# Attention scores in three bursts instead of four, value products together, and maxima turned at full width

## The chip, the cores and the metric

The kernel runs on one core of one Trainium2 chip. The time is the device time of one execution in microseconds (us). The median of three executions is 664.26 us, with 659.87 and 670.34 as the ends. One of its executions was also recorded by the hardware profiler; all rows below are from that one.

## The reference, cut to what matters

Two layers are computed on x of shape (4, 512, 512), fp32. The change is in the first one:

```python
xn = layernorm(x)
q = rope((xn @ wq).reshape(4, 512, 32, 16)); k = rope((xn @ wk).reshape(4, 512, 8, 16)); v = xn @ wv
scores = einsum('bqhd,bkhd->bhqk', q, repeat(k, 4)) / sqrt(16)   # causal mask added
s = einsum('bhqk,bkhd->bqhd', softmax(scores), repeat(v, 4)) @ wo
y_all = relu(einsum('bsd,edh->bseh', xn, W_e) + b_e)             # 8 experts, the top 2 of a token are used
x = x + s * silu(mean of the two chosen experts' rows)
```

There are 32 query heads and 8 key heads in each of 4 batches. The second layer (a long convolution and a linear gate) follows and is not touched.

## The kernel before, in words

**Groups.** The attention is done in 32 groups (b, h): one batch and one key head, with its 4 query heads. Group number i is 8b + h. The causal scores of a group are computed twice. The first time (`scores_1`, L1569, matmul L1591) they have the queries on the partitions, only so that the row maxima can be found; the second time (`scores_2`, L1596, matmuls L1617 and L1620) they have the keys on the partitions, with the negative maximum of each query added by two extra rows of the contraction, so that the exponential can be taken at once. Each of the two halves fills 10 PSUM banks' worth of work, n = 0 to 9. The first half goes round 3 banks (`S1_BANK`), the second round 3 others (`S2_BANK`). So `scores_1` number n may only start when the maxima of number n - 3 are out of the bank (the wait on `b_m`, L1584), and `scores_2` number n when the exponentials of number n - 3 are done (the wait on `b_e`, L1606). The contraction has 48 or 50 rows, and the two halves lie on different 64 rows of the array (`first_half` chooses them), so that one of each half can run side by side: a pair.

**Who does what.** VectorE takes the maxima (`maxima`, L1377, one L1390 instruction for each query head and tile, with a read of its accumulator behind it), turns the finished output of the group before (`rows_of`), divides it (`normalise`) and turns two groups' output for the projection (`pair_rows`). It also turns the expert tiles' gathered tokens (`expert_x`, L1458) and does a share of the second layer's preparation (`dve_s4`). ScalarE does the exponentials (`exps`, L1514) and the experts' relu (L1524). GpSimd zeroes the masked part of the diagonal blocks (`select`, L1332) and gathers tokens.

**The maxima of a group** go a long way round. After the tenth bank of maxima VectorE makes two negated fp32r parts (`maxima_parts`, L1403 and L1405), TensorE turns them into the first bank set (`turn_maxima`, L1628, called T below), VectorE copies 32 rows out (`maxima_rows`, L1413), and two DMAs, one issued by SyncE and one by ScalarE (`maximum_rows`, L1315), put the rows under the queries. `scores_2` number 0 of that group waits for both (`b_mr`, L1601).

**The order on TensorE** is written out by hand in `go` of `pe_b` (L1700). In the loop turn of group g, `following` is g + 1 and `after` is g + 2. A burst is a row of pairs. Between bursts stand quarters: a quarter is one of the 4 contraction steps of an expert tile (`expert`, L1672) or an output projection (`project`, L1683), as two fp32 matmul instructions of 512 columns; the first quarter of an expert tile has a short bias matmul in front (L1670). All these use bank 7, so a new tile waits until ScalarE has emptied it (`bank_free`). Between bursts lie the gaps 0 to 4; how many quarters stand in each gap of each group is `SIZES`: 6 and 8 by turns.

```python
scores(e, (2, 3, 4), following, (0, 1, 2), (b, h));  quarters(b, h, 0)     # burst A
scores(e, (5, 6, 7), following, (3, 4, 5), (b, h));  quarters(b, h, 1)     # burst B
scores(e, (8, 9), following, (6, 7), (b, h))                               # burst C
values(e, b, h, 0);  quarters(b, h, 2);  turn_maxima(e, *following)
scores(e, (0, 1), after, (8, 9), (b, h));  quarters(b, h, 3)               # burst D
for j in ORDER[1:]: values(e, b, h, j)
quarters(b, h, 4)
```

`values` (L1644) multiplies the exponentials with the values; four matmuls of 32 output rows run side by side.

**The stacks.** Queries and keys of two groups at a time are loaded by 12 DMAs (`load_stacks`, L1308 and L1309), issued by SyncE in every odd h, in order behind the stores of expert tiles, the shuffles of tokens and `maximum_rows`. They wait until the scores of the current group are all issued and done (`b_s2`, L1292), because they overwrite its buffer, and are needed by `scores_1` number 0 in the last burst of the next group (`b_ld`, L1578). This is already so in the kernel before, and `load_stacks` itself is not in the diff.

Of the kernel before, what the change touches and what calls it, by code (L numbers as in the profile page):

```python
# [21 lines left out]
F32 = mybir.dt.float32  # L22
# [54 lines left out]
def times_of(k):  # L77

    return {UNITS[n][1]: 4 * (b * KV + h) + min(gap, 3) for (b, h, gap), quarters in WORK.items() for n, q in quarters
            if q == k and UNITS[n][0] == "x"}  # L80
# [7 lines left out]
def turns():  # L88

    first, last, at = times_of(0), times_of(KB - 1), {}  # L90
    for m in range(MT):
        t = first[m] - 2 + m if m < 2 else max(first[m] - 2, last[m - 2])
        t += -1 if t % 2 == 0 and (m < 2 or t > last[m - 2]) else t % 2 == 0
        assert t < first[m]
        at.setdefault((t // (4 * KV), t // 4 % KV, t % 4 // 2), []).append(m)
    return at
# [24 lines left out]
for _name, _n in (("ident", P), ("half", 1), ("eps", 1), ("minus", 1), ("mask", S), ("tri", P), ("cos", TPB * 8), ("sin", TPB * 8), ("s4", 16),  # L121
                  ("lower", E * E), ("i128", NT), ("i128m", MT + 1), ("tile", MT), ("iota", P), ("tilenum", TOPK * NT), ("part", 1), ("sel", E)):
# [6 lines left out]
def constants():  # L129
# [26 lines left out]
    put("minus", -1.0)  # L156
    put("sel", np.arange(E)[None, :] == p[:, None] % 32)
# [58 lines left out]
def build(nc, x_d, wq_d, wk_d, wv_d, wo_d, wg_d, bg_d, we_d, be_d, lam_d, p_d, q_d, vct_d, ct_d, bp_d, dd_d,  # L216
          step_d, wft_d, sc_d, bf_d, const_d, dft_d, out_d):
    ctx = ExitStack()
    with ctx:
# [56 lines left out]
        NAR = 18440  # L276
# [186 lines left out]
        def dve_a(e, st):  # L463
            v = nc.vector
            v.memset(ones_b[:, :], 1.0).then_inc(a_ones, 1)
            v.memset(be3[:, :], 0.0).then_inc(dve_steps, st.one())
            e.wait_ge(a_load, 16)
# [76 lines left out]
            def rope(b, u):  # L544
                if due(at := 4 * (nth(b, u) - 1)):
                    e.wait_ge(a_add[u % 2], at)
                if (b, u) == LAST:
# [4 lines left out]
                    maxima_rows(e, 0, 0)  # L552
# [23 lines left out]
            def sequence(b, more):  # L576
                for u in range(TPB):
# [5 lines left out]
                    if (b, u) == LAST:  # L583
                        maxima_parts(e, st, 0, 0)
# [38 lines left out]
            maxima_parts(e, st, 0, 1)  # L623
            maxima_rows(e, 0, 1)
            dve_experts(e, st)
            for n in (0, 1):
# [192 lines left out]
        def pool_a(e, st):  # L819
# [12 lines left out]
            def constant_columns():  # L832
# [3 lines left out]
                g.memset(kt[32:64].bitcast(F32), 1.0).then_inc(b_init, 1)  # L836
                e.wait_ge(b_init, 1)
                g.memset(kt[96:P].bitcast(F32), 1.0).then_inc(b_init, 1)
# [142 lines left out]
        def pe_a(e):  # L981
# [89 lines left out]
            scores(e, (0, 1), (0, 2), (), None)  # L1071
# [136 lines left out]
        m_parts = parts("m_parts", [P, 2, 2, HALF * TPB], "arena", used[0])  # L1208
        take([P, 2, 2, HALF * TPB])
        m_rows = take([P, P])[0:2 * 2 * HALF * TPB]  # L1210
# [100 lines left out]
        def maximum_rows(e, b, h, s):  # L1311
# [3 lines left out]
            e.dma_start(qt[at:at + 2, h // 2 % 2, h % 2].bitcast(F32), m_rows[8 * TPB // 2 * s:8 * TPB // 2 * (s + 1), :]).then_inc(b_mr, 16)  # L1315
# [57 lines left out]
        def first_half(n):  # L1373
# [871 lines left out]
```

## Time and profile before

| | |
|---|---|
| median of 3 executions | 664.26 us (659.87 to 670.34) |
| profiled execution, from its first to its last instruction | 663.2 us |
| TensorE busy | 627.2 us (95%) |
| VectorE busy | 552.0 us (83%) |
| ScalarE, GpSimd busy | 287.0 us (43%), 238.2 us (36%) |
| mean granted TensorE clock | 0.987 of full speed |

For the profiled execution the profile gives the span alone, no device time with what lies around it; the span lies inside the range of the three times, 1.1 us below their median. The groups fill roughly the time from 140 to 550 us; before them lie the projections and the routing of tokens, after them the second layer. "Busy" of TensorE counts from the start of a matmul to its modelled end, which overlaps the next one. So the distance between the starts of two matmuls is the better measure of what a piece costs.

### The profile page before, as it was taken

The page shows a single profiled execution, that of the slowest core. Times are in us where ns is not written, and L with a number is a line of the kernel's source. Part 1 is how long each engine was busy: PE and PEld are TensorE (multiplying, and loading weights), DVE is VectorE, ACT ScalarE, POOL GpSimd, SP SyncE. Part 2 cuts the span into 40 slices and gives each one's busy share as a digit, 9 for nine tenths or more (in the row PEclk, how much of TensorE's full clock was granted, in tenths as well). Part 3 has the DMA queues.
Part 4 walks back from the last instruction along what each step waited for, and adds up shares of the span by engine and source line. Part 5 has one row for each costly group of instructions (what it writes and reads, how often), then busy time and mean ns, then how long its engine had stood idle before and what let it go on. Part 6 is the DMA issues. An engine that isn't in the chain of part 4 may idle for free.

```text
span 663.2 us, 12226 instructions
## 1 busy us (share of the span) xinstructions
PE 627.2 (95%) x3565; PEld 338.9 (51%) x3565; DVE 552.0 (83%) x1788; ACT 287.0 (43%) x535; POOL 238.2 (36%) x364
## 2 busy tenths in 40 slices
PE   8999999998999999999999999999999999789997
PEld 5788784433433334433443344443444343478886
DVE  6698999869978888989888798897789975689994
ACT  4353325434434435444444444443455443444441
POOL 3777641333323212332221322322222115576620
PEclk9999999969989999999999999999999999899999
DMA  7599989889788564675954649667276527768842
GB/s 262 141 336 266 337 239 173 146 164 273 152 268 161 166 139 80 154 132 188 194 105 98 136 109 220 125 173 152 52 167 111 171 72 241 156 145 217 217 104 79
DMA packets 79902, 113.10 MB, mean 171 GB/s; under 512 B 9704, under 2 KB 42664, under 8 KB 79840
## 3 DMA queue, kind: packets, MB, share of 16 engines
q1 hardware_dynamic: 68098, 86.90, 53.5%
q0 software_dynamic: 6704, 18.62, 11.8%
q10 hardware_dynamic: 5038, 6.84, 4.2%
q8 instruction: 29, 0.48, 0.3%
q14 instruction: 33, 0.27, 0.2%
HBM read 72.15 MB, written 39.65 MB: 169 GB/s over the span
## 4 chain that ended last, share of the span: by engine, by line
PE 55%; DVE 25%; DMA 8%; issue 4%; SPq 3%; POOL 2%; ACT 1%; ACTq 0%; DVEq 0%; POOLq 0%
PE bank L1672 13%; DVE bank L1390 12%; PE bank L1023 8%; PE bank L1591 7%; PE bank L2162 6%; PE bank L1644 5%; PE bank L1683 4%; PE bank L2167 4%; DMA w_e<-expert_rows,slots 3%; PE bank L1617 3%; DVE arena L1390 2%; DMA qt<-arena 2%; DMA qt<-turned_parts 2%; DVE m_parts L1403 2%; DVE m_parts L1405 1%
## 5 line engine op out<-in xcount | busy, mean ns | idle before, releaser
L1390 DVE CUSTOM_DVE_ANT_0 bank<-bank,cst 128x384 f32<-128x384 f32 (+3 forms) x512 | 234.9, 521 | 47.6 <-PE bank L1591 44.5
L1514 ACT ACTIVATE arena<-bank 128x512 f32<-128x512 f32 x320 | 170.9, 599 | 180.2 <-PE bank L1617 149.7
L1332 POOL TENSOR_SCALAR_AFFINE_SELECT arena<-arena 128x512 f32<-128x512 f32 x128 | 80.7, 643 | 309.2 <-ACT arena L1514 309.2
L1672 PE MATMUL bank<-w_e,arena 128*128 x312 | 162.2, 626 | 0.0
L1591 PE MATMUL bank<-kt,qt 48*128 48x512 f32 (+1 forms) x496 | 111.0, 338 | 5.6 <-DVE arena L1390 5.0
L1591 PEld LDWEIGHTS bank<-kt,qt 48*128 48x128 f32 x496 | 70.1, 187 | 83.9 <-DVE arena L1390 51.7
L1617 PE MATMUL bank<-qt,kt 50*128 50x512 f32 x256 | 88.2, 452 | 2.4 <-DMA qt<-arena 2.0
L1644 PE MATMUL bank<-arena 128*32 128x512 f32 (+3 forms) x1024 | 84.8, 445 | 0.4 <-ACT arena L1514 0.4
L1672 PEld LDWEIGHTS bank<-w_e,arena 128*128 128x128 f32 x312 | 54.6, 193 | 58.0 <-issue 54.3
L1390 DVE DVE_READ_ACCUMULATOR2_ANT arena<- 128x1 f32 x512 | 71.9, 140 | 0.0
L1683 PE MATMUL bank<-w_proj,arena 128*128 128x512 f32 x128 | 67.6, 636 | 0.0
L1023 PE MATMUL bank<-proj_high,xh 128*128 128x264 f32 (+1 forms) x128 | 46.1, 360 | 0.4 <-DVE xl L523 0.4
L1617 PEld LDWEIGHTS bank<-qt,kt 50*128 50x128 f32 x256 | 41.6, 186 | 7.5 <-DMA qt<-arena 2.9
L1524 ACT ACTIVATE arena<-bank 128x512 f32<-128x512 f32 x39 | 23.4, 600 | 49.7 <-PE bank L1672 49.7
L1644 PEld LDWEIGHTS bank<-arena 128*32 128x32 f32 x1024 | 24.3, 109 | 38.3 <-issue 24.5
L1023 PE MATMUL bank<-proj_high,xl 128*128 128x264 f32 (+1 forms) x128 | 43.4, 339 | 0.0
L1023 PE MATMUL bank<-proj_low,xh 128*128 128x264 f32 (+1 forms) x128 | 43.4, 339 | 0.0
L855 POOL TENSOR_TENSOR s_tok<-arena 128x256 f32<-128x256 f32 (+1 forms) x64 | 33.6, 558 | 26.2 <-DVE arena L542 20.8
L1344 POOL DMA_INDIRECT s_tok<-xn_rows,slots_i x39 | 37.3, 955 | 10.0 <-ACT arena L1514 4.1
L1683 PEld LDWEIGHTS bank<-w_proj,arena 128*128 128x128 f32 x128 | 21.3, 193 | 27.2 <-issue 24.9
L1912 POOL DMA_INDIRECT w_e<-expert_rows,slots x16 | 27.3, 1703 | 13.9 <-DMA w_e<-expert_rows,slots 9.7
L538 DVE TENSOR_TENSOR arena<-bank,cst 128x128 f32<-128x128 f32 (+1 forms) x63 | 27.1, 475 | 5.6 <-PE bank L1023 5.4
(167 smaller groups left out, 942.7 us busy)
## 6 DMA issues: line engine op xcount, KB each, us to landing
qt<-turned_parts SPq DMA_DIRECT2D x96, 128.0 KB, 4.7
turned_parts<-qk_parts SPq DMA_DIRECT2D x8, 1280.0 KB, 7.2
gathered_rows<-s_tok SPq DMA_DIRECT2D x39, 256.0 KB, 5.3
arena<-gathered_rows SPq DMA_DIRECT2D x39, 256.0 KB, 3.4
expert_rows<-arena SPq DMA_DIRECT2D x39, 256.0 KB, 4.5
w_e<-in_L_ffn_W_e ACTq DMA_DIRECT2D x24, 256.0 KB, 6.2
kt<-turned_parts SPq DMA_DIRECT2D x96, 64.0 KB, 4.4
arena<-in_L_attn_x SPq DMA_DIRECT2D x16, 256.0 KB, 6.1
```

What stands on the lines that cost most here:

```text
L855: i = g.tensor_tensor(o[:, :, :, c, :], xc[:, :, :, c, :], xs[:, :, :, 1 - c, :], op)
L1023: i = t.matmul(out[u % 2][:, 0:n], x[:, u % 2, k, :], w[part][:, k, :], start=(k == 0 and x is xh and part == 0), stop=(k == KB - 1 and pa ...
L1332: g.affine_select(out=diag, in_=diag, compare_op=ALU.is_ge, fill=0.0, base=0, pattern=[[0, 2], [0, HALF], [1, P]], channel_multiplier=-1). ...
L1344: e.indirect_dma_start(xr[m % 3], None, xn_d, bass.IndirectOffsetOnAxis(ap=slots_i[:, m:m + 1], axis=0)).then_inc(m_x[m % 3], 16)
L1390: i = v.tensor_tensor_reduce(out=part, in0=part, in1=const("mask")[:, S - w:], scale=1.0, scalar=LOWEST, op0=ALU.add, op1=ALU.max, accum_o ...
L1514: nc.scalar.activation(pt[:, s, first:second + 1:second - first].rearrange("p c r q -> p c (r q)"), s2_bank(b, h, n).rearrange("p (c x) -> ...
L1591: i = t.matmul(s1_bank(b, h, n)[:, at:at + w], stack[rows, x if r is None else r, q * P:w], kt[rows, h // 2 % 2, h % 2, 0:w], start=(x == ...
L1617: i = t.matmul(to, keys(j), queries[:, q:q + 2], start=True, stop=True)
L1644: i = nc.tensor.matmul(bank[4][VW * r:VW * (r + 1), j * P:], vb[:, j, h, :], pt[:, r // HALF, at:at + TPB - j, r % HALF, :], start=(j == O ...
L1672: i = t.matmul(bank[7], xgt[:, m % 2, k * P:(k + 1) * P], w_e[:, ex[m], k, :], start=False, stop=(k == KB - 1))
L1683: i = t.matmul(bank[to], ot[:, (b * PAIRS + k) % (PAIRS + 1), u, :], wo[:, k, :], start=(k == 0), stop=(k == KB - 1))
L2162: i = t.matmul(bank[2 + u % 2][:, :], x[:, u % 2, k, :], (w_high, w_low)[part][:, k, :], start=(k + n == 0), stop=(k + n == KB + 1))
```

## The change

- `SIZES` has 4 gaps instead of 5. The bursts have 4, 3 and 3 pairs: (3, 4, 5, 6) of `following` with (0, 1, 2, 3), then (7, 8, 9) with (4, 5, 6), then (0, 1, 2) of `after` with (7, 8, 9). The groups have 6, 8, 8 and 6 quarters in turn: BACK (2, 2, 2, 0), EIGHT (2, 4, 2, 0), EIGHT, FRONT (2, 3, 1, 0). The sum over four groups, 28, is that of before.
- All four value products stand together behind gap 2.
- T moves to gap 1, behind its third quarter at the latest (`TURN_AFTER`).
- VectorE no longer makes two parts before T. It copies the raw maxima into columns of a 128-wide tile (`maxima_columns`), which is turned at full width into the bank of the values (bank 4). The turned tile is then split in two full-width instructions, a rounded copy and a multiply-add. The constant rows of the keys become -1.
- On VectorE `normalise` stands before the copy of the turned maxima and `expert_x` behind it; `pair_rows` stands between. Before, `expert_x` stood ahead of it and the division behind the next group's first maxima.
- On SyncE `maximum_rows` stands ahead of the stores of expert tiles; on ScalarE it stands ahead of the relu of gap 1 and of the seventh exponential where gap 1 has 4 quarters.
- `turns` places the experts' transposes anew.

```diff
-GAPS = 5
+GAPS = 4
+TURN_AFTER = 3
-SIX, EIGHT = (2, 1, 1, 1, 1), (2, 2, 1, 1, 2)
+BACK, EIGHT, FRONT, SIX = (2, 2, 2, 0), (2, 4, 2, 0), (2, 3, 1, 0), (2, 2, 2, 0)
-SIZES = [NONE, (0, 0, 0, 2, 2)] + [SIX, EIGHT] * 12 + [SIX, SIX] + [SIX, EIGHT, (2, 2, 1, 1, 0), NONE]
+SIZES = [NONE, (0, 0, 2, 2)] + [BACK, EIGHT, EIGHT, FRONT] * 6 + [SIX, SIX] + [BACK, EIGHT, FRONT, NONE]
...
+        slots = [t for t in range(free, first[m]) if t % GAPS in (1, 2)]
+        t = max([t for t in slots if t < first[m] - 1] or slots)
...
+    put("less", -1.0 * (p // 8 % 8 == 1))
...
-                g.memset(kt[32:64].bitcast(F32), 1.0).then_inc(b_init, 1)
+                g.memset(kt[32:64].bitcast(F32), -1.0).then_inc(b_init, 1)
...
+        def turned_at(b, h):
+            return bank[(0, 1)[h] if b * NG + h < 2 else 4][:, 0:P]
...
-            v.tensor_scalar(m_parts[:, :, 0], rows, -1.0, None, ALU.mult).then_inc(dve_steps, st.one())
-            v.scalar_tensor_tensor(out=m_parts[:, :, 1], in0=rows, scalar=-1.0, in1=m_parts[:, :, 0].bitcast(F32),
-                                   op0=ALU.mult, op1=ALU.subtract).then_inc(b_mx, 1)
+        def maxima_columns(e, b, h):
+            e.wait_ge(b_m, nth_of(NJ, b, h, NJ))
+            nc.vector.tensor_copy(m_cols[:, :, 0:2], rows.unsqueeze(2).to_broadcast([P, 2, 2, HALF * TPB])).then_inc(b_mx, 1)
...
-            nc.vector.tensor_copy(m_rows, S1_BANK[nth_of(NJ, b, h, NJ + 2) % 3][0:2 * 2 * HALF * TPB, 0:P]).then_inc(b_me, 1)
+            v.tensor_copy(m_high[:, :], turned_at(b, h)).then_inc(dve_steps, st.one())
+            e.wait_ge(dve_steps, st.count())
+            v.scalar_tensor_tensor(out=m_rows[:, :], in0=m_high[:, :].bitcast(F32), scalar=const("less"), in1=turned_at(b, h),
+                                   op0=ALU.mult, op1=ALU.add).then_inc(b_me, 1)
... (dve_b)
-                        for n in (2, 3, 4):
+                        for n in (3, 4, 5, 6):
                             maxima(e, *following, n)
                     rows_of(*done)
-                        for n in range(5, NJ):
+                        for n in (7, 8, 9):
                             maxima(e, *following, n)
-                        maxima_parts(e, st, *following)
+                        maxima_columns(e, *following)
+                    if later:
+                        normalise(*done)
+                    if following:
+                        maxima_rows(e, st, *following)
+                    if later and done[1] % 2:
+                        pair_rows(done[0], done[1] // 2)
                     for m in TURNS.get((b, h, 0), ()):
                         expert_x(m)
-                        maxima_rows(e, *following)
-                        for n in (0, 1):
+                        for n in (0, 1, 2):
                             maxima(e, *after, n)
-                    if later:
-                        divided(*done)
... (act_b)
-                    for n in (0, 1, 2):
+                    for n in (0, 1, 2, 3):
                         exps(e, b, h, n)
                     results(b, h, 0)
-                    for n in (3, 4, 5):
+                    for n in (4, 5, 6):
                         exps(e, b, h, n)
+                    early = len(WORK[b, h, 1]) > TURN_AFTER
+                    if following and early:
+                        maximum_rows(e, *following, 1)
                     results(b, h, 1)
+                    exps(e, b, h, 7)
+                    if following and not early:
+                        maximum_rows(e, *following, 1)
... (scores_1, turn_maxima, values)
-            if n == 2 and due(at := nth_of(1, b, h, 0)):
-                e.wait_ge(b_me, at)
+            if n == 2 and b == 0 and h in (1, 2):
+                e.wait_ge(b_me, h)
+            if due(at := nth_of(1, b, h, -1)):
+                e.wait_ge(b_o, at)
+            t.transpose(turned_at(b, h), m_cols.rearrange("p s c x -> p (s c x)"), ident).then_inc(b_tm, 1)
+                if 0 < b * NG + h < NB * NG - 1:
+                    e.wait_ge(b_me, nth_of(1, b, h, 2))
... (pe_b)
+                    scores(e, (3, 4, 5, 6), following, (0, 1, 2, 3), (b, h))
                     quarters(b, h, 0)
+                    scores(e, (7, 8, 9), following, (4, 5, 6), (b, h))
+                    quarters(b, h, 1, 0, TURN_AFTER)
+                    turn_maxima(e, *following)
+                    quarters(b, h, 1, TURN_AFTER)
+                    scores(e, (0, 1, 2), after, (7, 8, 9), (b, h))
                     quarters(b, h, 2)
+                    for j in ORDER:
+                        values(e, b, h, j)
                     quarters(b, h, 3)
... (sp_b)
-                    stores(b, h, 0, 1)
                     shuffles(b, h, 0)
                         maximum_rows(e, *next_group(b, h, 1), 0)
+                    stores(b, h, 0, 1)
                         load_stacks(e, *next_group(b, h, 3))
```

## Rows read from the trace of the kernel before

**Rows 1.** Windows: engine busy in each stretch, then granted clock, DMA share, GB/s.

```profile
120.00:140.00 20.00, 17.75 (x103) 7.96 (x104) 16.64 (x65) 7.54 (x15) 9.67 (x12) 0.84 0.70 165
...
300.00:400.00 100.00, 95.98 (x564) 40.56 (x557) 84.55 (x313) 44.72 (x86) 26.69 (x38) 1.00 0.60 135
```

**Rows 2.** Lines by form, TensorE, 200 to 500 us: busy, mean ns, idle before.

```profile
L1628 PE MATMUL bank<-cst,m_parts 128*32 128x128 f32 x22 | 6.3, 284 | 7.3 <-DVE m_parts L1405 7.3
```

**Rows 3.** Waits: engine line, waited for, total us, times, longest.

```profile
PE bank L1628 <- DVE m_parts L1405: 11.1, 30, 1.3
...
PE bank L1591 <- DVE arena L1390: 5.0, 10, 0.8
```

**Rows 4.** Timeline of TensorE, one turn of the loop: start, us, engine line.

```profile
302.65 0.49 PE L1591 MATMUL bank<-kt,qt 48*128 48x512 f32 x1
...
303.56 0.39 PE L1670 MATMUL bank<-be,sel_e 128*128 128x512 bf16 x1
...
305.60 0.44 PE L1591 MATMUL bank<-kt,qt 48*128 48x384 f32 x1
...
306.55 1.98 PE L1672 MATMUL bank<-w_e,arena 128*128 x4
...
309.14 1.06 PE L1644 MATMUL bank<-arena 128*32 128x512 f32 x8
310.14 0.39 PE L1670 MATMUL bank<-be,sel_e 128*128 128x512 bf16 x1
...
311.58 0.28 PE L1628 MATMUL bank<-cst,m_parts 128*32 128x128 f32 x1 [0.20 <-DVE m_parts L1405]
311.80 0.50 PE L1591 MATMUL bank<-kt,qt 48*128 48x512 f32 x1
...
312.47 1.13 PE L1672 MATMUL bank<-w_e,arena 128*128 x2
313.53 1.54 PE L1644 MATMUL bank<-arena 128*32 128x256 f32 x24
315.00 1.98 PE L1672 MATMUL bank<-w_e,arena 128*128 x4
316.91 0.49 PE L1591 MATMUL bank<-kt,qt 48*128 48x512 f32 x1
```

**Rows 5.** Timeline of VectorE in the same turn and the next.

```profile
309.00 0.43 DVE L1390 CUSTOM_DVE_ANT_0 bank<-bank,cst 128x256 f32<-128x256 f32 x1 [0.47 <-PE bank L1591]
...
310.50 0.14 DVE L1390 DVE_READ_ACCUMULATOR2_ANT arena<- 128x1 f32 x1
...
310.98 0.55 DVE L1405 SCALAR_TENSOR_TENSOR m_parts<-arena,m_parts 128x16 fp32r<-128x16 f32 x1
...
312.08 0.24 DVE L1413 COPY arena<-bank 32x128 f32<-32x128 f32 x1
...
313.71 0.25 DVE L1428 RECIPROCAL arena<-arena 128x16 f32<-128x16 f32 x1
314.06 0.43 DVE L1432 TENSOR_TENSOR arena<-arena 128x256 f32<-128x256 f32 x1
...
317.55 0.70 DVE L1390 CUSTOM_DVE_ANT_0 bank<-bank,cst 128x512 f32<-128x512 f32 x1 [2.07 <-PE bank L1591]
```

**Rows 6.** Timeline of TensorE and VectorE, an A burst that found VectorE late.

```profile
176.43 0.49 PE L1591 MATMUL bank<-kt,qt 48*128 48x512 f32 x1
...
177.56 0.67 DVE L1390 CUSTOM_DVE_ANT_0 bank<-bank,cst 128x512 f32<-128x512 f32 x1
```

**Rows 7.** Timeline of SyncE queue: issues of one load of the stacks.

```profile
503.09 0.64 SPq L1315 DMA_DIRECT2D qt<-arena  x1
503.90 0.45 SPq L1308 DMA_DIRECT2D kt<-turned_parts  x1
```

**Rows 8.** Chain of waits, in order of time: start, us, what.

```profile
139.89 3.41 PE bank L1672 x4
...
510.60 4.82 DMA qt<-turned_parts
```

More of the change, by code:

```diff
@@ L77, in times_of @@
 def times_of(k):
-    return {UNITS[n][1]: 4 * (b * KV + h) + min(gap, 3) for (b, h, gap), quarters in WORK.items() for n, q in quarters
+    return {UNITS[n][1]: GAPS * (b * KV + h) + gap for (b, h, gap), quarters in WORK.items() for n, q in quarters
             if q == k and UNITS[n][0] == "x"}
@@ L91, in turns @@
     for m in range(MT):
[L92 to L95, printed above, removed]
+        free = last[m - 2] if m > 1 else GAPS
+        slots = [t for t in range(free, first[m]) if t % GAPS in (1, 2)]
+        t = max([t for t in slots if t < first[m] - 1] or slots)
+        at.setdefault((t // (GAPS * KV), t // GAPS % KV, t % GAPS - 1), []).append(m)
     return at
@@ L121 @@
 for _name, _n in (("ident", P), ("half", 1), ("eps", 1), ("minus", 1), ("mask", S), ("tri", P), ("cos", TPB * 8), ("sin", TPB * 8), ("s4", 16),
-                  ("lower", E * E), ("i128", NT), ("i128m", MT + 1), ("tile", MT), ("iota", P), ("tilenum", TOPK * NT), ("part", 1), ("sel", E)):
+                  ("lower", E * E), ("i128", NT), ("i128m", MT + 1), ("tile", MT), ("iota", P), ("tilenum", TOPK * NT), ("part", 1), ("sel", E), ("less", 1)):
     COLS[_name] = (_at, _at + _n)
@@ L466, in dve_a @@
             v.memset(be3[:, :], 0.0).then_inc(dve_steps, st.one())
+            v.memset(m_cols, 0.0).then_inc(dve_steps, st.one())
             e.wait_ge(a_load, 16)
@@ L1070, in pe_a @@
                 values(e, 0, 0, j)
-            scores(e, (0, 1), (0, 2), (), None)
+            scores(e, (0, 1, 2), (0, 2), (), None)
             keep_awake(6, bank[2])
@@ L1207, in build @@
         row_max = take([P, R, TPB])
-        m_parts = parts("m_parts", [P, 2, 2, HALF * TPB], "arena", used[0])
-        take([P, 2, 2, HALF * TPB])
-        m_rows = take([P, P])[0:2 * 2 * HALF * TPB]
+        m_cols = take([P, 2, 8, HALF * TPB])
+        m_high = parts("m_high", [P, P], "arena", used[0])
+        take([P, P])
+        m_rows = parts("m_rows", [P, P], "arena", used[0])
+        take([P, P])
         rsum = take([P, QB])
@@ L1685, in project, with quarters @@
                     i.then_inc(b_p, 1)
-            def quarters(b, h, gap):
-                for n, k in WORK[b, h, gap]:
+            def quarters(b, h, gap, first=0, end=None):
+                for n, k in WORK[b, h, gap][first:end]:
                     kind, at = UNITS[n]
```

57 lines of the change are left out of this document (17 added, 40 removed).

## The prediction, made before the changed kernel was run

> **What bounds the kernel now.** I looked first at the windows. In 300 to 400 us, wholly inside the groups, TensorE is busy 96% at full granted clock, VectorE 85%, and the DMA engines 60% [rows 1]. So the groups are bound by TensorE, with VectorE close behind. The lines by form give 22 turns (T) in 300 us [rows 2]: 13.64 us a group. Then the waits: TensorE stood idle 11.1 us before T, for VectorE's parts of the maxima, and 5.0 us before first-half scores, for the maxima in their bank [rows 3]. That is all an edit of waiting can win there, 16 us of 663. The rest must come from what TensorE's own work costs, so I read its timeline from one A burst to the next [rows 4], start to start, since busy times overlap. I take 29 groups with the full pattern.
>
> **TensorE's own work.** In the turn shown (8 quarters, 302.65 to 316.91, 14.26 us) [rows 4]: A is 0.91 (to 303.56), B 0.95 (305.60 to 306.55), D 0.67 (311.80 to 312.47). C lies in the 2.59 from 306.55 to 309.14 with two quarters; two quarters alone are 1.91 (315.00 to 316.91), so C is 0.68. A third pair costs 0.24, and a burst 0.2 beyond its pairs. One quarter is 1.06 (312.47 to 313.53), two are 1.91: 0.86 each and 0.2 for each row of quarters. Switching between whole-array quarters and the half-array pairs thus costs 0.2 on either side. Values are 1.00 (309.14 to 310.14) and 1.47 (313.53 to 315.00); eight instructions of 512 columns pass in 0.86 by the quarter's rate, so 0.14 of the first piece is entry and exit. T is 0.22 (311.58 to 311.80).
>
> New turn with the same 8 quarters: A 1.16, two quarters 2.04 (303.56 to 305.60, with bias matmul), B 0.95, three quarters 2.78 + 0.12 bias, T 0.22, one quarter 1.06, C 0.91, two quarters 1.91, values 2.33: 13.5. The old one without its T wait of 0.26 is 14.0. So 0.5 is saved with 8 quarters. With 6 quarters, or in FRONT with 7 around it, T does not split a row of quarters: 0.7. Mean 0.6 x 29 = **-17 us**. Bounds: 0.35 if the merged values save nothing and T, now 128 columns of weights wide, costs as much as a quarter's entry more (-10); 0.7 everywhere (-20).
>
> **The waits that go.** T now waits for one short copy instead of two dependent instructions (the second alone 0.55 [rows 5]), and stands behind two or three quarters instead of one quarter. With three quarters TensorE reaches T at B + 0.95 + 2.9 = B + 3.85. VectorE can start bank 7 at 0.64 (316.91 to 317.55), takes 0.78 a bank (309.00 to 310.64 for two) and I allow 0.4 for the columns: B + 3.4. Hidden. With two quarters (BACK) T waits 0.5, but BACK follows FRONT and that wait is swallowed by the load wait below. The turned tile no longer uses a score bank, so the five us before scores go too: **-16 us** together [rows 3]; at least -11.
>
> **VectorE's total** hardly moves. Out go 0.27 + 0.55 + 0.24; in come a copy of 32 columns, a full-width copy from PSUM and a full-width multiply-add. No row shows a 128x128 one; bounds are 0.24 (the 32-row copy) and 0.55 (the fp32r multiply-add) [rows 5]. I take 0.25 and 0.4, the middle for the second, as it is like both. With a gap for the dependence, the turned rows are ready 0.7 after `normalise`. By the Trainium skill, "VectorE: DVE Perf Modes", the errata section, an instruction with a PSUM source costs 120 cycles plus one for each element of a partition, whatever the number of partitions, 0.26 us here for either; by that the second is 0.14 shorter and the sum some 1 us lower.
>
> **New wait one: the fourth pair of burst A.** Each half has three banks. Score 6 waits for the maxima of score 3, and the second half's score 3 for exponential 0, both of the same burst. In the trace an A burst starts at 316.91 and an idle VectorE starts on it at 317.55 for 0.70 [rows 4, 5], with 0.06 for the accumulator read's tail: free at A + 1.4. In unbroken flow the fourth pair would start at A + 0.8. Wait 0.6, x 29 = **+17 us**. Bounds: 0.3, if it hides what the end of a burst costs (+9); 1.1, as where an A burst at 176.43 found VectorE busy until 177.56 [rows 6] (+32). I take 0.6, for between C and A VectorE has 5.2 us (C 0.91, two quarters, values) + 0.64, and its work there is at most three banks (2.0), `dve_s4` (1 to 2) and one or two transposes (0.7 each).
>
> **New wait two: the stacks.** Their 12 DMAs take from 503.90 to the last landing at 510.60 + 4.82 = 515.42: 11.5 us [rows 7, 8]. They start behind burst C of an odd h and must land before burst C of the next group. Before, that interval held 7 quarters always. Now behind FRONT it holds 1 + 2 + 2 = 5. TensorE's flow: C 0.91, quarter 1.06, values 2.33, A 1.16 + 0.6, two quarters 2.04, B 0.95, two quarters 1.91, T 0.22 + 0.5 = 11.7. The loads cannot start at C + 1.0, where the scores end: SyncE first waits in `maximum_rows`. Columns at B + 3.4, `normalise` 0.78 (313.71 to 314.49 [rows 5]), rows 0.7: B + 4.9, which is C + 0.85, as C starts at B + 4.05. Its issue takes 0.64 [rows 7], and in half of the cases a store follows: C + 1.5 to 2.0, landing at C + 13.2. Wait 1.5, in groups 5, 9, 13, 17, 21, 25; behind 27 (6 quarters) 0.7. **+10 us**. Bounds: 0.8 each if SyncE is free at C + 1.0 (+5); 2.5 each with another us of contention (+16). Behind EIGHT the interval has 8 quarters and hides it.
>
> **Small ones.** In EIGHT ScalarE issues `maximum_rows` (0.64) before it empties bank 7 behind gap 1, while TensorE needs the bank 0.91 later, behind C: about 0.15 x 13 = **+2**, at most +6. From T to burst A the rows' DMAs have 6.5 us in EIGHT, 5.4 in BACK and 4.6 in FRONT; it was 5.3 (311.58 to 316.91 [rows 4]), and no wait for them is among the long ones there: nothing, at most 0.7 x 7 = +5. `expert_x` behind the maxima's copy keeps a late token load off that path, which the start could gain from; I count nothing. `pair_rows` and `normalise` are moved, not added. GpSimd's selects must be in before the values, which come later than before: hidden.
>
> **Sum:** -17 - 16 + 17 + 10 + 2 = -4. The profiled span is 663.2, so 659.2; the median of the runs is 1.1 above that span: **660 us**. Two waits of the new order eat what the fewer switches give.
>
> **Rivals.**
> 1. **Only the gains.** ScalarE and VectorE answer within the burst, and the loads start at C + 1.0: A wait 0.3, load wait 0.8. -20 - 16 + 9 + 5 + 1 = -21: 643. For it: VectorE's total is 85%, and all switches are dear. Against: three banks, and an answer of 1.4 us [rows 5]. Chance 0.25.
> 2. **VectorE falls behind (slower).** Place: maxima of score 3 in burst A. Where the work since C is over 5.9 us, burst A waits its excess, T behind it again, since T's slack is 0.45. `turns` puts two transposes into one slot in FRONT groups, and one into each slot in many EIGHT ones. If half the groups lose 1.1 more, +16, with T waiting 0.5 in them, +7: 660 + 23 = 683. It decides from some 0.5 us of lag on. For it: the row at 176.43, where a transpose stood ahead. Against: VectorE stood idle 2.07 before 317.55 [rows 5]. Chance 0.10.
> 3. **The clock falls.** A low stretch shows in 120 to 140 us (mean 0.84) [rows 1], and four matmul instructions, two quarters, then take 3.41 instead of 1.91 [rows 4, 8], at the lower of the two levels. If each of the seven load waits were followed by two quarters at that level, 7 x 1.5 x 2 = +21: 681. The Trainium skill, "TensorE: Matmul & The Clock Gate", in "A second HAM failure mode: psum-queue depth-cycling", says that frequent short idling between groups of matmuls as they go round their banks makes the clock fall and rise; by that rule this change, with its wait in every A burst, would be slower. Against it in the trace: the granted clock stays 1.00 with 30 waits of up to 1.3 us at T [rows 1, 3]. Chance 0.05.
> 4. **It does not do what it says:** T is not the wait but the bank, and the fourth pair takes its place one for one, with no load wait: 660 - 10 = 650, inside my forecast's spread.
>
> My forecast has 0.60: its own range is 648 to 672. Rival 1 lies at 643 with 637 to 650, the slow rivals at 675 to 690. The range for 8 in 10 is 642 to 677. A measurement of this kernel can tell about 2% from no change, that is below 651 and above 677.5. Faster: rival 1's 0.25 and a little of the forecast, 0.28. Slower: 0.13. Within: 0.59.
>
> **What would show it.** After: T idle nearly gone; a wait of TensorE before first-half scores for L1390's successor, some 29 times 0.5 to 0.7 us, at the fourth pair of A; six waits of 1 to 2 us for the stacks' DMAs at burst C, every fourth group; group periods near 14.0, 14.0, 13.0 and 13.3; bursts of 1.75, 0.95 and 0.91 and one piece of values of 2.3. The prediction is wrong if the fourth pair follows at once, if the loads land in time behind FRONT, or if VectorE's idle before burst A is gone.

## The result, and the profile after

The changed kernel takes 686.72 us (median of 4 runs, 680.97 to 689.34); the kernel before, run beside it, 665.4 us (659.87 to 670.34). The ratio is 1.0299, 95% interval 1.0258 to 1.0341: 3% slower. The forecast was 660 us with a range of 642 to 677.

| | before | after |
|---|---|---|
| span of the profiled execution | 663.2 us | 683.3 us |
| TensorE busy | 627.2 us (95%) | 617.3 us (90%) |
| VectorE busy | 552.0 us (83%) | 551.2 us (81%) |
| mean granted TensorE clock | 0.987 | 0.969 |

The work is the same or less; TensorE stands idle. The windows of the kernel after answer to [rows 1] (columns: the stretch and its length, then busy us of TensorE, its weight loads, VectorE, ScalarE, GpSimd, the granted clock, DMA share, GB/s):

```profile
200.00:300.00 100.00, 87.76 (x512) 40.11 (x514) 78.09 (x289) 40.73 (x79) 25.56 (x36) 0.95 0.61 130
300.00:400.00 100.00, 86.80 (x486) 40.33 (x488) 80.93 (x302) 41.95 (x80) 26.39 (x37) 0.96 0.60 131
400.00:500.00 100.00, 90.53 (x532) 41.97 (x537) 79.83 (x298) 42.23 (x81) 24.22 (x36) 0.98 0.57 129
```

TensorE is busy 87 to 91 us of each 100, where it was 96 to 97, VectorE 78 to 81 where it was 85 to 87, and the clock is no longer full. Both engines wait for something else. The waits of the kernel after, against [rows 3] (engine line, waited for, total us, times, longest):

```profile
PE bank L1601 <- DMA qt<-turned_parts: 20.6, 8, 4.1
PE bank L1601 <- DVE arena L1399: 13.1, 32, 1.2
...
PE bank L1640 <- DVE arena L1408: 6.9, 12, 2.3
...
PE bank L1683 <- ACT arena L1532: 4.2, 10, 0.5
```

L1601 is the first-half score matmul (L1591 before), L1640 the turn T (L1628), L1399 the maxima (L1390), L1683 the bias matmul. The top row is the largest part of the loss: eight waits for the stacks. The start of each T shows where the time goes: in the turn of group 2 T comes at 156.91 against 155.91 before, in the turn of group 5 at 202.21 against 201.54, in the turn of group 29 at 550.54 against 528.71. The start of the loop costs nothing; 21.2 of the 21.8 us are lost between the turns of groups 5 and 29.

**A turn without a load wait** (TensorE timeline of the kernel after: start, us, engine line; EIGHT, to be laid beside [rows 4]):

```profile
298.22 0.50 PE L1601 MATMUL bank<-kt,qt 48*128 48x512 f32 x1
...
299.57 0.44 PE L1601 MATMUL bank<-kt,qt 48*128 48x384 f32 x1 [0.33 <-DVE arena L1399]
...
300.01 1.98 PE L1685 MATMUL bank<-w_e,arena 128*128 x4
301.92 0.45 PE L1601 MATMUL bank<-kt,qt 48*128 48x384 f32 x1
...
303.10 2.74 PE L1685 MATMUL bank<-w_e,arena 128*128 x6 [0.16 <-issue]
305.68 0.27 PE L1640 MATMUL bank<-cst,arena 128*128 128x128 f32 x1
305.79 1.02 PE L1685 MATMUL bank<-w_e,arena 128*128 x2
306.74 0.50 PE L1601 MATMUL bank<-kt,qt 48*128 48x512 f32 x1
...
308.19 0.39 PE L1683 MATMUL bank<-be,sel_e 128*128 128x512 bf16 x1 [0.47 <-ACT arena L1532]
...
310.22 2.36 PE L1657 MATMUL bank<-arena 128*32 128x512 f32 x32
312.51 0.49 PE L1601 MATMUL bank<-kt,qt 48*128 48x512 f32 x1
```

A is 1.79 start to start (298.22 to 300.01), with the fourth pair late by the wait for maxima; values are 2.29 in one piece (310.22 to 312.51); T costs 0.11 between two quarters (305.68 to 305.79). In FRONT turns, where T stands in front of burst C, it costs 0.20 (202.21 to 202.41). C with what follows is 1.45 (306.74 to 308.19), 0.47 of it a wait for the relu.

**A turn with a load wait** (the same view, behind FRONT, group 6; T, then burst C):

```profile
211.42 1.98 PE L1685 MATMUL bank<-w_e,arena 128*128 x4
213.68 0.33 PE L1640 MATMUL bank<-cst,arena 128*128 128x128 f32 x1 [0.27 <-DVE arena L1408]
217.83 0.79 PE L1601 MATMUL bank<-kt,qt 48*128 48x512 f32 x1 [3.82 <-DMA qt<-turned_parts]
...
219.41 0.61 PE L1683 MATMUL bank<-be,sel_e 128*128 128x512 bf16 x1
219.81 3.62 PE L1685 MATMUL bank<-w_e,arena 128*128 x4
```

TensorE stands still for 3.8 us, and the two quarters behind burst C cost 3.55 (219.81 to 223.36, where the values begin) instead of 1.91: the clock has fallen. The windows of the low stretches show how far, beside a stretch of the load itself (the same columns as above):

```profile
217.20:224.10 6.90, 6.27 (x16) 2.46 (x20) 3.47 (x9) 1.68 (x3) 1.23 (x2) 0.51 1.06 289
278.70:282.10 3.40, 3.40 (x8) 0.78 (x10) 3.23 (x8) 0.91 (x2) 2.17 (x3) 0.50 0.15 19
...
209.00:218.00 9.00, 4.91 (x21) 2.19 (x21) 6.14 (x27) 2.46 (x5) 1.66 (x3) 0.96 1.05 174
```

0.50 is the lower level, 1.2 GHz. Such stretches begin at 217.2, 278.7, 336.7, 394.7 and 456.2, each at or within 2 us behind a load wait, and these waits are 3.8, 2.9, 4.1, 3.4 and 2.7 us long; two of the stretches last 6.8 us, three 3.4. Behind the last two load waits, of 2.2 and 1.3 us, there is none. From the start of burst C to the next T these five cases take 15.60, 14.20, 14.31, 15.74 and 14.32 us; the same pieces behind the wait of 1.3 us, at full clock, take 12.68 (537.86 to 550.54). So the low clock costs about 11 us in all.

The loop has a sixth low stretch, at 159.2 in the turn of group 2, and the kernel before has one, at 191.5. Both begin at a much shorter pause, and neither pause is one for the stacks (TensorE timelines, first the kernel after, then the kernel before):

```profile
159.67 3.44 PE L1685 MATMUL bank<-w_e,arena 128*128 x4 [1.21 <-DVE arena L1464]
```

```profile
190.99 0.50 PE L1617 MATMUL bank<-qt,kt 50*128 50x512 f32 x2 [1.32 <-DMA qt<-arena]
```

During the load itself the DMA share is 1.05: the 16 engines are full.

**The load's time.** SyncE's queue (start, us, issue), then the same load's last transfer in the chain of waits:

```profile
203.22 0.62 SPq L1320 DMA_DIRECT2D qt<-m_rows  x1
203.88 0.40 SPq L1785 DMA_DIRECT2D expert_rows<-arena  x1
204.45 0.49 SPq L1313 DMA_DIRECT2D kt<-turned_parts  x1
...
210.27 0.42 SPq L1314 DMA_DIRECT2D qt<-turned_parts  x1
```

```profile
210.27 7.52 DMA qt<-turned_parts
```

Burst C of group 5's turn began at 202.41, so the first issue at 204.45 is C + 2.0, as forecast. But the last byte lands at 217.79: the load takes 13.3 us, not 11.5. The first five loads behind FRONT take 13.3, 12.8, 13.9, 13.4 and 13.1; those of the kernel before took 10.7 to 12.5, median 11.5. What else is on the DMA engines then, GpSimd's timeline says:

```profile
205.09 1.17 POOL L1349 DMA_INDIRECT s_tok<-xn_rows,slots_i  x1
...
209.22 0.95 POOL L1349 DMA_INDIRECT s_tok<-xn_rows,slots_i  x1
```

Two gathers of tokens start inside the load. In the kernel before, in the same group's load, one did, at 209.47, and the other had gone at 201.61. All five of these loads have two gathers inside. The times of the gathers come out of the quarters' order, which the new `SIZES` changed. The gathers' number is not all of it: the loads with one gather inside took 11.9 to 13.1 us in the changed kernel and 10.7 to 12.5 in the kernel before. What else lengthened those is not shown. On the queue of the gathers the packets took 12.7% of 683.3 us, 87 us of all 16 engines, against 11.8% of 663.2 or 78 before, for the same 6704 packets (page, part 3: queue, packets, MB, share):

```profile
q0 software_dynamic: 6704, 18.62, 12.7%
```

**The turned rows** (VectorE timeline, against [rows 5]):

```profile
304.89 0.18 DVE L1408 COPY arena<-arena 128x32 f32<-128x32 f32 x1
...
305.99 0.29 DVE L1416 CAST m_high<-bank 128x128 fp32r<-128x128 f32 x1 [0.29 <-PE bank L1640]
306.32 0.35 DVE L1418 SCALAR_TENSOR_TENSOR m_rows<-m_high,cst,bank 128x128 fp32r<-128x128 f32 x1
```

0.29 and 0.35 where I took 0.25 and 0.4. By the formula of the Trainium skill, "VectorE: DVE Perf Modes", the errata section, either is estimated at 0.26: the first agrees within 0.03, the second is 0.09 longer.

### The profile page after: what moved, and what is told of

The parts are those of the page before. It is cut to its first block, busy times and chain, and to the rows that moved or that the text cites. A ratio compares the mean times of both kernels' runs of the same rounds, so it can differ in the third digit from the quotient of the medians.

```text
span 683.3 us, 12195 instructions
## 1 busy us (share of the span) xinstructions
PE 617.3 (90%) x3541; PEld 351.0 (51%) x3565; DVE 551.2 (81%) x1789; ACT 285.4 (42%) x535; POOL 239.5 (35%) x364
## 3 DMA queue, kind: packets, MB, share of 16 engines
q0 software_dynamic: 6704, 18.62, 12.7%
## 4 chain that ended last, share of the span: by engine, by line
PE 52%; DVE 16%; DMA 13%; SPq 8%; issue 5%; POOL 2%; ACT 2%; ACTq 2%; DVEq 0%; POOLq 0%
PE bank L1685 16%; PE bank L1657 8%; DMA qt<-turned_parts 7%; DVE bank L1399 6%; PE bank L2173 6%; PE bank L1601 6%; PE bank L1696 4%; PE bank L2178 4%; PE bank L1026 3%; DMA turned_parts<-qk_parts 3%; SPq L1313 3%; SPq L1314 3%; DMA w_e<-expert_rows,slots 3%; PE bank L1627 1%; DVE m_rows L1418 1%
## 5 line engine op out<-in xcount | busy, mean ns | idle before, releaser
L1399 DVE CUSTOM_DVE_ANT_0 bank<-bank,cst 128x384 f32<-128x384 f32 (+3 forms) x512 | 234.3, 523 | 68.8 <-PE bank L1601 66.6
L1685 PE MATMUL bank<-w_e,arena 128*128 x312 | 156.8, 628 | 5.3 <-issue 4.0
L1601 PE MATMUL bank<-kt,qt 48*128 48x512 f32 (+1 forms) x496 | 110.9, 340 | 33.0 <-DMA qt<-turned_parts 20.6
L1601 PEld LDWEIGHTS bank<-kt,qt 48*128 48x128 f32 x496 | 68.9, 189 | 100.9 <-DVE arena L1399 43.8
L1627 PE MATMUL bank<-qt,kt 50*128 50x512 f32 x256 | 95.1, 455 | 0.4 <-ACT arena L1522 0.4
L1685 PEld LDWEIGHTS bank<-w_e,arena 128*128 128x128 f32 x312 | 57.6, 198 | 52.1 <-issue 48.0
L1657 PE MATMUL bank<-arena 128*32 128x512 f32 (+3 forms) x1024 | 78.7, 445 | 0.0
L1399 DVE DVE_READ_ACCUMULATOR2_ANT arena<- 128x1 f32 x512 | 72.0, 141 | 0.0
L1657 PEld LDWEIGHTS bank<-arena 128*32 128x32 f32 x1024 | 28.4, 111 | 55.3 <-issue 46.9
L1627 PEld LDWEIGHTS bank<-qt,kt 50*128 50x128 f32 x256 | 45.1, 188 | 4.2 <-ACT arena L1522 3.3
L858 POOL TENSOR_TENSOR s_tok<-arena 128x256 f32<-128x256 f32 (+1 forms) x64 | 33.6, 558 | 26.1 <-DVE arena L545 20.4
L1349 POOL DMA_INDIRECT s_tok<-xn_rows,slots_i x39 | 38.8, 994 | 10.9 <-ACT arena L1522 3.8
L1696 PEld LDWEIGHTS bank<-w_proj,arena 128*128 128x128 f32 x128 | 23.0, 199 | 25.8 <-issue 21.6
```

What stands on the lines that cost most here:

```text
L858: i = g.tensor_tensor(o[:, :, :, c, :], xc[:, :, :, c, :], xs[:, :, :, 1 - c, :], op)
L1349: e.indirect_dma_start(xr[m % 3], None, xn_d, bass.IndirectOffsetOnAxis(ap=slots_i[:, m:m + 1], axis=0)).then_inc(m_x[m % 3], 16)
L1399: i = v.tensor_tensor_reduce(out=part, in0=part, in1=const("mask")[:, S - w:], scale=1.0, scalar=LOWEST, op0=ALU.add, op1=ALU.max, accum_o ...
L1601: i = t.matmul(s1_bank(b, h, n)[:, at:at + w], stack[rows, x if r is None else r, q * P:w], kt[rows, h // 2 % 2, h % 2, 0:w], start=(x == ...
L1627: i = t.matmul(to, keys(j), queries[:, q:q + 2], start=True, stop=True)
L1657: i = nc.tensor.matmul(bank[4][VW * r:VW * (r + 1), j * P:], vb[:, j, h, :], pt[:, r // HALF, at:at + TPB - j, r % HALF, :], start=(j == O ...
```

## The experiments

**The theory.** The loads stretch over the two gathers, TensorE waits 21 us for them, and each wait is followed by a stretch at the lower clock. **Rivals:** the late relu in EIGHT is a second cause of its own; the fourth pair of A costs more than its 0.6; the clock would have fallen anyway.

The first four ran beside one kernel before (664.42 us, 7 runs), the next four beside another set (666.06, 9 runs), the last two beside a third (665.52, 11 runs).

### 1. The load behind eight quarters

```diff
-SIZES = [NONE, (0, 0, 2, 2)] + [BACK, EIGHT, EIGHT, FRONT] * 6 + [SIX, SIX] + [BACK, EIGHT, FRONT, NONE]
+SIZES = [NONE, (0, 0, 2, 2), (2, 2, 0, 0)] + [BACK, EIGHT, EIGHT, FRONT] * 7 + [NONE]
```

> The changed kernel with its cycle of quarters moved by one group (group 2 has 4 quarters, then BACK, EIGHT, EIGHT, FRONT seven times), so that the interval of 5 quarters no longer lies on a load of the stacks; the loads' intervals hold 8 and 7 quarters. Theory 'short interval' (the stacks' load behind FRONT is what was mis-sized, and it brings the low clock): the seven waits of 1.4 to 4.2 us at the C burst fall to 0.5 or less, the granted clock in 200 to 500 us is 1.00, and the time is 24 to 30 us below the changed kernel's, about 658 us, a ratio to the kernel before of 0.985 to 0.995. Rival 'DMA load' (the loads are slower because everything moves closer together, wherever the quarters stand): waits for the stacks stay, 2 us or more in most of the odd groups, time within 8 us of the changed kernel's, ratio 1.02 to 1.03. Rival 'fourth pair does it' : same, ratio about 1.03.

Measured: 670.47 us (668.62 to 676.53), ratio 1.0108, interval 1.0043 to 1.0173. The waits for the stacks halve:

```profile
PE bank L1601 <- DMA qt<-turned_parts: 10.0, 9, 2.8
```

What was left stands mostly in the interval that now begins in an EIGHT turn, ends in a FRONT turn and holds seven quarters, because the loads still took 12.0 to 14.4 us (T of one such turn at 214.62, TensorE's timeline):

```profile
216.71 0.50 PE L1601 MATMUL bank<-kt,qt 48*128 48x512 f32 x1 [1.81 <-DMA qt<-turned_parts]
```

Low stretches between 200 and 560 us fall from five to two. With the same order inside the turn, 16 us come back between the medians (1.9% by the ratios, 13 us) by a shift of which turn is short. The place of the loss is right; 24 to 30 were expected, so the load's length was not yet understood.

### 2. The relu ahead of the maximum rows

```diff
+                    results(b, h, 1)
                     if following and early:
                         maximum_rows(e, *following, 1)
-                    results(b, h, 1)
```

> The changed kernel with one undone order on ScalarE: where gap 1 has 4 quarters, the relu (or copy) of bank 7 comes before the issue of the maxima's rows. Theory: the 0.5 us wait of the bias matmul behind burst C in the twelve EIGHT groups goes, burst C there takes 0.91 instead of 1.41, and the time falls by 5 to 6 us (0.8%), ratio about 1.02. Rival: the rows' DMA is then late, burst A waits in its second half, and the time is the same (ratio 1.03).

Measured: 685.39 us (676.89 to 688.45), ratio 1.0324, interval 1.0273 to 1.0375. The wait of 0.5 us behind C is gone from the trace (C is 0.90 in EIGHT), and the time is not shorter. That missed what I expected. The trace is of the shortest execution, 676.89; the other three, 683.28 to 688.45, are as long as those of the changed kernel. With runs 11 us apart it decided nothing; experiments 9 and 10 ask again.

### 3. TensorE kept busy through the wait

```diff
                     quarters(b, h, 1, TURN_AFTER)
+                    if (b * NG + h) % 2 == 0 and WORK[b, h, 1] and len(WORK[b, h, 1]) == 2:
+                        e.wait_ge(b_e, nth_of(NJ, b, h, 5))
+                        keep_awake(10, s2_bank(b, h, 7))
                     scores(e, (0, 1, 2), after, (7, 8, 9), (b, h))
```

> The changed kernel with ten idle bf16 matmuls of 512 columns (2.1 us) on TensorE ahead of burst C in the even groups with two quarters in gap 1 (2, 6, 10, ... 26, 28), where it otherwise waits for the stacks. Theory 'low clock is a follow-on of the wait': the granted clock stays 1.00 in 200 to 500 us, the waits for the stacks are shorter by these 2.1 us but burst C begins no later, and the time falls by 8 to 10 us, ratio about 1.016. Rival 'the clock falls for another reason' : still the low stretches every fourth group, time equal to the changed kernel's or 2 to 4 us more, ratio 1.03.

`keep_awake` multiplies a tile of ones into a bank that the next score overwrites. Measured: 677.31 us (673.86 to 679.37), ratio 1.0172, interval 1.0121 to 1.0224. The same turn as above (TensorE timeline):

```profile
213.86 0.33 PE L1640 MATMUL bank<-cst,arena 128*128 128x128 f32 x1 [0.27 <-DVE arena L1408]
214.03 2.32 PE L982 MATMUL bank<-ones_b 128*128 128x512 bf16 x10
217.78 0.49 PE L1601 MATMUL bank<-kt,qt 48*128 48x512 f32 x1 [1.44 <-DMA qt<-turned_parts]
...
218.92 1.88 PE L1685 MATMUL bank<-w_e,arena 128*128 x4
220.73 2.36 PE L1657 MATMUL bank<-arena 128*32 128x512 f32 x32
```

Burst C starts at the same moment (217.78 against 217.83), yet the two quarters take 1.81 instead of 3.55. Of the five low stretches one is left, at 268.1, behind a wait of 1.3 us for the maxima in the fourth pair. Nothing else was touched, so about 9 of the lost us are the clock's (9.4 between the medians, 8.5 by the ratios), and behind these waits the clock falls because TensorE stands still.

### 4. Burst A as three pairs, a quarter, one pair

```diff
-                    scores(e, (3, 4, 5, 6), following, (0, 1, 2, 3), (b, h))
-                    quarters(b, h, 0)
+                    scores(e, (3, 4, 5), following, (0, 1, 2), (b, h))
+                    quarters(b, h, 0, 0, 1)
+                    scores(e, (6,), following, (3,), (b, h))
+                    quarters(b, h, 0, 1)
```

> The changed kernel with burst A cut in two: three pairs, one quarter, the fourth pair, the other quarters of gap 0. The banks are free by then. Theory 'fourth pair waits 0.6': A with its two quarters takes 0.91 + 1.06 + 0.44 + 1.06 = 3.47 instead of 1.78 + 1.91 = 3.69; 0.2 x 27 groups, of which the load wait takes back that behind FRONT: 3 to 5 us less, ratio 1.023 to 1.027. Rival 'VectorE is what sets the pace, not the burst': the wait comes back at T or at burst B, time the same.

Measured: 684.56 us (683.39 to 687.83), ratio 1.0291, interval 1.0251 to 1.033. From the start of A to burst B it is now 3.50 instead of 3.70 (298.22 to 301.92 above), and the waits for maxima before first-half scores fall from 13.1 to 1.4 us. The time hardly moves. The waits for the stacks stay, with seven low stretches between 200 and 560 us instead of five, and the waits at T rise from 6.9 to 8.6 us, which is a part of what the rival said:

```profile
PE bank L1601 <- DMA qt<-turned_parts: 20.1, 8, 3.5
```

My reading is that a gain of TensorE's flow between two loads is lost at the next load, whose end is set by the DMA engines. This experiment alone does not separate that from the clock and the waits at T; experiment 8 asks again.

### 5. The gathers ahead of the load

```diff
-        gathered.setdefault((q // 2, 0) if q > 1 and q % 2 else (max(q // 2 - 1, 0), 2), []).append(m)
+        g, slot = (q // 2, 0) if q > 1 and q % 2 else (max(q // 2 - 1, 0), 2)
+        gathered.setdefault((g, 0) if g % 2 else (g, slot), []).append(m)
```

> The changed kernel with the token gathers of odd groups moved ahead of the load of the stacks (GpSimd issues them after its first select of the group and no longer after its last). In the changed kernel 160 packets of gathers fall into each load behind FRONT, two tiles; in the kernel before 80 to 105. Theory 'two gathers on the load': the loads behind FRONT take 11.5 to 12 us instead of 12.8 to 13.9, their wait falls from 3.5 to about 1.8 us, some low stretches of the clock go too, and the time falls by 10 to 15 us: ratio 1.008 to 1.015. Rival 'the load is slow for its own packets': its duration stays at 13 us and the time within 3 us of the changed kernel's, ratio about 1.03.

Measured: 674.51 us (672.58 to 678.18), ratio 1.0141, interval 1.0089 to 1.0194. GpSimd's timeline, and TensorE behind T of the same turn:

```profile
197.48 0.95 POOL L1350 DMA_INDIRECT s_tok<-xn_rows,slots_i  x1
...
209.74 0.94 POOL L1350 DMA_INDIRECT s_tok<-xn_rows,slots_i  x1 [0.15 <-issue]
```

```profile
214.18 0.33 PE L1641 MATMUL bank<-cst,arena 128*128 128x128 f32 x1 [0.26 <-DVE arena L1409]
216.55 0.49 PE L1602 MATMUL bank<-kt,qt 48*128 48x512 f32 x1 [2.04 <-DMA qt<-turned_parts]
```

The load goes from 204.95 to 216.51, 11.6 us with one gather inside instead of 13.3 with two; the next ones behind FRONT take 11.2, 12.8, 11.5, 11.4 and 11.6, with none or one inside. The waits fall to 11.9 us, near what the forecast had said they would be (10), and the queue of the gathers is back to 11.6% of 670.8 us, 78 us as before:

```profile
PE bank L1602 <- DMA qt<-turned_parts: 11.9, 7, 3.1
```

The kernel is still 1.4% slower than the one before. The loads' length is the largest part of the miss and not all of it: two low stretches are left between 200 and 560 us, and the waiting at T is 6.8 us as it was.

### 6. The uneven quarters in the kernel before

```diff
-SIZES = [NONE, (0, 0, 0, 2, 2)] + [SIX, EIGHT] * 12 + [SIX, SIX] + [SIX, EIGHT, (2, 2, 1, 1, 0), NONE]
+SIZES = [NONE, (0, 0, 0, 2, 2)] + [SIX, EIGHT, EIGHT, (2, 2, 1, 1, 0)] * 6 + [SIX, SIX] + [SIX, EIGHT, (2, 2, 1, 1, 0), NONE]
```

> The kernel before with nothing changed but the quarters: 6, 8, 8 and 6 in turn instead of 6 and 8, so that the interval of every second load of the stacks holds 5 quarters instead of 7, as in the changed kernel. Theory 'the short interval alone': every fourth group waits 1 to 3 us for the stacks at burst D, some low stretches of the clock follow, and the time rises by 6 to 18 us: ratio 1.01 to 1.027. Rival 'only together with the new bursts': no such waits, ratio 1.00.

Measured: 675.79 us (671.5 to 681.71), ratio 1.0121, interval 1.0059 to 1.0183. The waits are those of an execution of 681.7 us, the longest of the four; the ratio leaves it out.

```profile
PE bank L1591 <- DMA qt<-turned_parts: 6.9, 4, 2.5
```

The old order of bursts, with quarters laid out as in the change, loses 8 us (interval 4 to 12) of the change's 20. A good third of the loss does not need the new bursts; the rest is not seen there.

### 7 and 8. All three put right, then burst A split too

Experiment 7 is the edits of 1, 2 and 5 together; experiment 8 adds that of 4.

> The changed kernel with three repairs together: the cycle of quarters moved by one group, the relu of bank 7 ahead of the maxima's rows, and the gathers moved off the loads. Theory: with the cycle moved 670; the waits for the stacks in the 7-quarter intervals (2 to 3 us every fourth group) fall to under 1 us, and the relu's 0.5 us in the EIGHT groups now counts: 655 to 661 us, ratio 0.985 to 0.995. Rival: another wait takes their place (VectorE before T and at the fourth pair): 666 to 670, ratio 1.00 to 1.01.

> The kernel with the three repairs together, and burst A cut in two as well (three pairs, one quarter, the fourth pair, the rest of gap 0). Theory 'fourth pair waits 0.6, a further burst costs 0.4': 0.2 x 27 = 5 us less than without the cut, now that no wait for the stacks takes it back; 650 to 656 us, ratio 0.978 to 0.988. Rival 'VectorE sets the pace': equal to the kernel without the cut.

Measured: 660.35 us (659.6 to 663.99), ratio 0.9913, interval 0.9879 to 0.9947, for experiment 7; 652.22 us (650.85 to 654.01), ratio 0.9782, interval 0.9736 to 0.9828, for experiment 8. Its windows and its wait for the stacks:

```profile
200.00:300.00 100.00, 95.81 (x585) 43.50 (x586) 85.88 (x321) 47.67 (x89) 27.35 (x40) 1.00 0.72 152
300.00:400.00 100.00, 96.96 (x565) 44.28 (x564) 86.92 (x334) 47.83 (x90) 27.73 (x40) 0.98 0.67 138
```

```profile
PE bank L1602 <- DMA qt<-turned_parts: 5.6, 5, 1.7
```

Both came out as expected. TensorE is as full as before the change, with less to do. The split that showed nothing in experiment 4 is worth 8.1 us here, where 5 were expected. A part of the 8.1 is the clock's: between 200 and 560 us the trace of experiment 7 has three low stretches, that of experiment 8 one. With the repeats below in place of experiment 8 it is 5 us.

### 9 and 10. The relu again, now that no load wait hides it

Experiment 10 is the kernel of experiment 8 once more; experiment 9 is the same with the relu behind the maximum rows, as the change has it.

> The version that was 2.2% faster than the kernel before (loads behind eight quarters, gathers moved ahead of the load, burst A split), but with the maximum rows issued ahead of the bank's relu again, as in the changed kernel. The open question is whether that issue costs anything in the time: alone its move showed none, while load waits and the clock still filled the slack. Theory: with the load waits gone nothing swallows it, so the 0.5 us in each of 12 to 14 EIGHT groups, +6 us, ratio to before 0.984 to 0.990. Rival: TensorE's wait at the bias matmul lets VectorE and ScalarE catch up, so it is only moved; then the ratio stays at 0.976 to 0.981.

> The same version as the one that was 2.2% faster, once more, with the relu first, as the partner of the run with it late: ratio 0.974 to 0.982. Under the theory it is 6 us below its partner, under the rival within 2 us of it.

Measured: 653.8 us (653.51 to 655.07), ratio 0.9835, interval 0.9814 to 0.9856, with the relu late; 653.94 us (651.11 to 658.85), ratio 0.9836, interval 0.9801 to 0.9871, with it first. Both ratios lie outside what was expected, but the two are equal: the 6 us of the theory are ruled out, a difference of up to 3 us is not. The wait is there in experiment 9, and absent from experiment 10:

```profile
PE bank L1684 <- ACT arena L1533: 3.2, 7, 0.5
```

The rival's outcome holds, its mechanism only in part. The traces show where the half microseconds go. From the values at 322.43 to those at 416.12 experiment 9 takes 93.69 us; experiment 10 takes 91.72 for the same turns (325.49 to 417.21). The relu first does shorten the turns between two waits for the stacks, by 1.6 to 2.0 us in each of three such stretches. Most of it is lost where TensorE waits for a DMA, as here at the same burst C (TensorE timelines, experiment 9, then experiment 10, with a low stretch at 322.8 that experiment 9 does not have):

```profile
320.47 0.49 PE L1602 MATMUL bank<-kt,qt 48*128 48x512 f32 x1 [1.03 <-DMA qt<-turned_parts]
```

```profile
322.29 0.50 PE L1602 MATMUL bank<-kt,qt 48*128 48x512 f32 x1 [1.83 <-DMA qt<-turned_parts]
```

From T in the turn of group 5 to T in that of group 29 the two take 319.17 and 318.23 us. The repeat also puts the best version at 1.6 to 2.2% faster than the kernel before, not surely 2.2.

## Why the prediction was wrong

The forecast was -4 us in all. For the 24 turns between the T of group 5's turn and that of group 29's its terms make about 0: +2 for TensorE's own work with the fourth pair and the relu, -11.4 for the waits that go (8.3 at T and 3.1 before scores, in the trace of before), +9.7 for the stacks. Measured in these turns is +21.2. The steps, one by one:

- **TensorE's own work (-17): right in its pieces.** A 1.79 with its wait (1.76 forecast), values 2.29 (2.33), C 0.91. One piece I had not seen: T at full width costs 0.11 between two quarters. In front of a burst it costs 0.20, as much as before (0.22).
- **The fourth pair (+17): right.** 1.79 - 1.16 = 0.63 in most turns, and up to 1.7 in single ones. The list of waits shows mostly 0.33 of it as TensorE's idle; where the rest lies is not traced.
- **The waits that go (-16): partly.** 6.9 us of waiting at T are left. Of these 2.9 lie ahead of group 5's turn, outside the stretch that lost time; 1.9 stand ahead of load waits (0.27 seven times) and cost nothing of their own. Only the 2.1 in groups 8, 16 and 24 are lost in the stretch. VectorE is late there: the three quarters and T take 3.56 instead of 2.57.
- **The stacks (+10): the step that failed.** Mechanism, place and start (C + 2.0) were as written, and so was TensorE's flow of 11.7 (202.41 to 213.9 is 11.5). The duration was not. I took 11.5 us from one load of the kernel before, and nearly any of its loads would have given that: four with no gather started inside took 11.1 to 11.5, nine with one 10.7 to 12.5. The mistake was to carry the number over without asking what the new `SIZES` does to `GATHERED`, which is worked out from it. The loads with two gathers inside took 12.8 to 13.9. Seven waits of 1.3 to 4.1 us make 20.4, where the term had 10. Experiment 5 moves the gathers and comes near the forecast's number: 11.9. My upper bound, 2.5 each "with another us of contention", stopped at +16.
- **The clock (0 in the sum, a rival at 0.05): the second failure.** I left it out because the clock "stays 1.00" through waits of up to 1.3 us at T. That was misread: before, the clock had fallen at 191.5, behind a wait of 1.32 us at 190.99, and the mean of 140 to 200 us was 0.94. The sum itself held load waits of 1.5, and no row showed that those were harmless. The rival's price was also worked out wrongly: two quarters at the lower level cost 1.5 more, so seven waits make 10.5, and the factor 2 behind it has no source. Experiment 3 measures 9 us, the trace 11. This rival should have stood on the load's term, as a second price of it, and not beside it. The Trainium skill, "TensorE: Matmul & The Clock Gate", in "A second HAM failure mode: psum-queue depth-cycling", lays such falls on many short pauses while banks are cycled. The trace agrees only in that idling goes ahead of a fall: the 0.33 us pause before the fourth pair came in nearly every turn, but each of the six low stretches of the loop had a single pause of 1.2 to 4.1 us at its start or less than 2 us ahead of it.
- **The relu (+2): the wait was 0.5, not 0.15.** It cost less than 3 us of the time when the load waits were small (experiments 9 and 10).

Together, for the 24 turns: load waits 20.4, low clock 11, waits at T and before scores -7.3 (4.1 left of 11.4), smaller waits of the kernel before that are gone -1. The rest, TensorE's own work with the fourth pair and the relu, is what remains to 21.2, -2. Against the forecast the stacks are 11 us longer, the clock 11, the waits at T 4, and the own work and small waits 4 shorter. Of rival 2, a late VectorE, 2 to 3 us came true. Rival 1, only the gains, was wrong for this kernel; experiment 8, with its repairs, comes near its range of 637 to 650: 652, and 654 when repeated.

The prediction's spread was also too narrow by its own account: the load term and the clock term stand on the same event, and both go the same way. 675 to 690 held 0.15 by my chances.

## What to carry to other kernels

When a table of work is changed, follow everything that is computed from it, the issue times of transfers too, and look what each large load will share the DMA engines with. A wait of TensorE can cost more than its length: here 20.4 us of waits for the stacks brought some 9 to 11 us of low clock. Add to a wait what the following quarters take at the lower clock, and treat the two as one term. And a gain between two waits for a transfer shows only when the transfer is early enough: the split gave nothing alone (experiment 4) and 5 to 8 us after the loads had room.

## What the runs showed of the hardware

- Of the waits for the stacks between 200 and 560 us, in the traces of all runs, each of the ten of 2.85 us or more had a low stretch (0.50 of the clock, 3.4 or 6.8 us long) at it or less than 2 us behind it. So had eleven of the thirteen of 2.0 to 2.83 us, and five of the twenty-three of 1.0 to 1.83 us. Single waits of 1.2 and 1.3 us for something else went ahead of a fall too (159.2 in the changed kernel, 191.5 in the one before). So no length of wait divides the cases. With ten matmuls of ones in the pause, and 1.44 us idle behind them, the level held.
- With the DMA engines full (share 1.05 around the load), a load of 12 transfers took 13.3 us with two gathers of 128 rows inside and 11.6 with one (group 5, changed kernel and experiment 5); in groups 9 and 17 it took 12.8 and 13.4 with two and 11.2 and 11.5 with none.
- A full-width fp32 transpose between two whole-array matmuls took 0.11 us of TensorE's time; in front of a burst it took 0.20, as much as the narrow one of 32 columns in the kernel before (0.22).
